# GpSimd's gathers wait for pair n - 10 in place of pair n - 16, in a two-pass graph kernel

## The chip, the cores and the metric

The kernel runs on one core of one Trainium2 chip. The metric is the device time of one execution in microseconds (us). Three runs of the kernel before are shown; their median is 2636.99 us. A pass of the kernel takes some 1250 us, so times of single waits are given to hundredths of a us.

## The reference, cut to what matters

Two graph layers run one after the other over 6250 nodes and 106250 edges, all vectors with 256 float32 elements. An edge has a source and a destination node; the edges are sorted by destination. Only the message part of each layer matters here:

```python
# layer 0, the first pass
msg = relu(x[src] + edge_attr)
agg = segment_sum(msg, dst)          # then a dense part per node, giving x
# layer 1, the second pass
h = gelu((x[src] + edge_attr) @ W1m + b1m)
agg = segment_sum(h @ W2m + b2m, dst) / max(degree, 1)   # then a dense part per node
```

## The kernel before, in words

**Tiling.** A group is 1024 edges: 8 tiles of 128, in 4 pairs of tiles. There are G = 104 groups, so M = 416 pairs; a pair is numbered n, and n = 4 g + j for pair j of group g. A round is 16 pairs. Both passes go over all pairs, and the code of each engine is written pair by pair: `first_pass(i, s)` and `second_pass(i, s)` hold what the engine does at pair 16 i + s, with the dense work on nodes (`node_a`, `node_b`) laid between the pairs by tables. The first rounds and the last ones are written out, those between are a loop.

**A pair in the first pass.** GpSimd gathers the 2 x 128 rows x[src] from memory into a slot of `m_all` with two indirect DMAs (`gather`, its instruction is L682), one for each tile; the first eight pairs take their indices from a list that is there early. SyncE loads the edges' attributes into `e_all` (L559). ScalarE copies them to a PSUM bank (L848). VectorE adds bank and gathered rows in place (`add_edges`, L1537) and raises the semaphore `added`. ScalarE applies the relu (L858). TensorE multiplies the two tiles by selection matrices to sum them by destination (`tile_sums`, L1141), and raises `pair_summed` by 2 after the pairs with j = 1 and j = 3. Beside it TensorE makes some of the second pass's products ahead (`ahead`, L1174), which ScalarE keeps (L867, L872). Who waits for `pair_summed` in this pass: ScalarE before it keeps these products and copies the sums (L918), VectorE before it makes the selection matrices of the group after the next in order (L1457) and before it adds a group's sums to `acc` (L1487), SyncE before it loads `ez` (L562), and GpSimd.

**A pair in the second pass.** GpSimd gathers rows of `y_scratch`, which the first pass has stored (y is x @ W1m + b1m of the new x), into the same slots. TensorE multiplies the edges' attributes by W1m (`product`, L1215) for j = 0, 1, 2 and raises `z_made` after each; for j = 2 (second tile) and j = 3 ScalarE copies stored products (`put_z`, L888). VectorE adds gathered rows to the bank (`add_rows`, L1560, raises `added`), ScalarE makes the gelu twice (L910, L911), VectorE the low part (L1566), and TensorE sums (`sums_split`, L1257), four pairs behind the products. `z_made` is waited for by VectorE's addition, by `put_z` and by SyncE's loads of edges (L540). Three pieces of products of the last groups are made early too, in this pass (`make_early`, L1227).

**The ring of gathered rows.** `m_all` has ROUND = 16 slots and one semaphore `m_in` for each. Before a gather of pair n goes into a slot, what was in it must have been used. In the first pass the slot is free when the sums of pair n - 16 are done; GpSimd waits for `pair_summed` >= n - 15. In the second pass the slot is free when pair n - 16 has been added; GpSimd waits for `added` >= M + n - 15. So up to sixteen pairs are gathered or in flight ahead of the sums (of the additions, in the second pass). The eight pairs 0 to 7 are gathered before the other lists are there, and pairs 8 to 15 without a wait for sums. At the start of the second pass GpSimd waits for the last y, and before pair 12 also for `xab_out` and `a_clear`, since the last slots are used by the dense work of the first pass.

**GpSimd's other work.** After the gathers of each pass it makes a few reciprocal square roots for the last nodes (`deviation`, L706 and L708). VectorE waits for them.

Of the kernel before, what the change touches and what calls it, by code (L numbers as in the profile page):

```python
# [23 lines left out]
BLK = 2  # L24

ROUND = 16
PER_ROUND = ROUND // PAIRS
ERING = 8
AHEAD = 3
# [57 lines left out]
def rounds(eng, body, first, stop, last):  # L87

    for i in range(first):
        for s in range(ROUND):  # L90
            body(i, s)
    with eng.Fori(0, stop - first) as r:
        for s in range(ROUND):
            body(r + first, s)
    for n in range(stop * ROUND, last + 1):
        body(n // ROUND, n % ROUND)


def groups(eng, body, first, stop):

    for i in range(first):
        for q in range(PER_ROUND):
            body(i, q)
    with eng.Fori(0, stop - first) as r:
        for q in range(PER_ROUND):
            body(r + first, q)


def known(n):
    return isinstance(n, int)  # L110


def build(nc, x, xT, src, dst, edge, edgeT, w1T, w2T, w1m, w2mT, w1u, w2u, vt, vr, out):
# [4 lines left out]
    M = G * PAIRS  # L118
# [9 lines left out]
    TURN = 512 - (KD + 1) * WIN  # L128
    assert P <= repeated < 2 * P and M == ROUND * ROUNDS and G > full and KH == 2 * KD and G <= P and CHUNK % 2 == 0 and N % 4 == 2
    assert ENDING < left and left - ENDING <= P  # L130

    chunks = [(c * CHUNK, CHUNK) for c in range(R)] + [(R * CHUNK, left - ENDING), (N - ENDING, ENDING)]

    need = [PER_ROUND * (c + 1) + 1 for c in range(R)] + [G - 1, G]
    LOOP_A, LOOP_B = (3, ROUNDS - 1), (4, ROUNDS - 1)
# [19 lines left out]
    def last_group(places, i, s):  # L155

        found = [G - LAST_SUMS + e for e, n in enumerate(places) if known(i) and n is not None and M + n == i * ROUND + s]
        return divmod(found[0], PER_ROUND) if found else None

    def ending(c):  # L160
        return known(c) and c >= R
# [20 lines left out]
    def groups_needed(c):  # L182
        return need[c] if known(c) else PER_ROUND * c + PER_ROUND + 1

# [14 lines left out]
    with ExitStack() as ctx:  # L199
# [134 lines left out]
        def small_b(c):  # L334
            return small_l if known(c) and c == R - 1 else small(c)
# [14 lines left out]
        def row(name, rows, blocks):  # L350
# [18 lines left out]
        added, act_made, act_high, act_low, z_made = map(sem, ("added", "act_made", "act_high", "act_low", "z_made"))  # L369
        sel_made, pair_summed, sum_copied, sum_turned, acc_done = map(  # L370
            sem, ("sel_made", "pair_summed", "sum_copied", "sum_turned", "acc_done"))
# [52 lines left out]

        ends_by_psum = PER_ROUND * (ROUNDS - 1)

# [73 lines left out]
        def tile_of(i, s):  # L500

            return 1 if known(i) and ROUND * i + s == M - PAIRS else 0
# [173 lines left out]
        @block.gpsimd  # L676
        def _(pool):
            def gather(table, sources, n, first=0):
                g, j = divmod(n, PAIRS)
                for t in range(first, 2):  # L680
                    u = 2 * j + t
                    pool.indirect_dma_start(  # L682
                        out=m_sb[n % ROUND][:, t, :], out_offset=None, in_=table,
                        in_offset=bass.IndirectOffsetOnAxis(ap=sources(g, u), axis=0),
                    ).then_inc(last_in if n == M - 1 and t == 0 else m_in[n % ROUND], 16)

            pool.iota(iota_i[:], pattern=[[1, WIN]], base=0, channel_multiplier=0).then_inc(consts_made, 1)
            pool.iota(place[:], pattern=[[1, 1]], base=0, channel_multiplier=1).then_inc(consts_made, 1)
            pool.memset(ident[:], 0.0).then_inc(consts_made, 1)
            pool.memset(eps[:], EPS).then_inc(consts_made, 1)  # L690
            pool.memset(root[:], -0.5).then_inc(consts_made, 1)
            pool.wait_ge(consts_made, 5)
            pool.affine_select(out=ident[:], in_=ident[:], compare_op=ALU.not_equal, fill=1.0, base=0,
                               pattern=[[-1, P]], channel_multiplier=1).then_inc(consts_made, 1)
            pool.wait_ge(src_first, 16)
            for n in range(2 * PAIRS):
                gather(x, lambda g, u: src_0[:, g, u:u + 1], n)
            pool.wait_ge(lists_made, 2)
            for n in range(2 * PAIRS, M):
                if n >= ROUND:  # L700
                    pool.wait_ge(pair_summed, n - ROUND + 1)
                gather(x, lambda g, u: src_p[:, u, g:g + 1], n)

            def deviation(m, rows, at, n):

                pool.tensor_tensor(m.ve[0:rows, at], m.mv[0:rows, at, 1], eps[0:rows, at], ALU.add).then_inc(eps_added, 1)  # L706
                pool.wait_ge(eps_added, n)
                pool.tensor_tensor(m.rs[0:rows, at], m.ve[0:rows, at], root[0:rows, at], ALU.pow).then_inc(rooted, 1)  # L708

            def deviation_x(e, at, steps, n):  # L710

                pool.wait_ge(x_dev[e], steps)
                deviation(small_x[e], chunks[R + e][1], slice(at, at + 1), n)

            rows = CHUNK // BLK
            pool.wait_ge(a_dev, DEV_A * (R - 1) + 2)
            deviation(small_n, rows, slice(0, BLK), 1)
            deviation_x(0, 0, 2, 2)
            deviation_x(1, 0, 2, 3)

            pool.wait_ge(lists_made, 4)
            pool.wait_ge(pair_summed, M)
            pool.wait_ge(y_out, 16 * C)
            for n in range(M):
                if n == 12:

                    pool.wait_ge(xab_out, 32 * C)
                    pool.wait_ge(a_clear, C)
                if n >= ROUND:
                    pool.wait_ge(added, M + n - ROUND + 1)  # L730
                gather(y_dram, lambda g, u: src_u[:, u, g:g + 1], n, tile_of(*divmod(n, ROUND)))

            for k, (c, second) in enumerate(roots):
                if ending(c):
                    deviation_x(c - R, second, 9 if second else 6, 4 + k)
                    continue
                pool.wait_ge(last_dev[c - R + 2], 5 if second else 2)
                at = slice(BLK, 2 * BLK) if second else slice(0, BLK)
                if c == R - 2 and second:
                    pool.wait_ge(b_o, c)  # L740
                elif c == R - 2:

                    pool.wait_ge(b_dev, DEV_B * (R - 2))
                    pool.wait_ge(b_o, c - 1)
                    at = slice(0, 2 * BLK)
                deviation(small_b(c), rows, at, 4 + k)
# [1162 lines left out]
```

## Time and profile before

| | us |
|---|---|
| median of the 3 runs (2627.64 to 2640.62) | 2636.99 |
| the profiled execution | 2636.03 |
| its span, first to last instruction | 2634.2 |
| busy: TensorE / GpSimd / VectorE / ScalarE | 2019.9 / 1593.8 / 1496.7 / 1290.4 |
| mean granted share of TensorE's clock | 0.898 |

The first pass runs from about 29 us to 1285 us of the span, the second from 1285 us to the end. In rows of the timeline the first number is the start, the second the time taken, then the engine (PE is TensorE, DVE VectorE, ACT ScalarE, POOL GpSimd, SPq the issuing of a DMA by SyncE), line, operation, what it writes and reads, shape and how many instructions were merged. In brackets stands how long the engine had been idle before it and what ended that wait; "remote" is a semaphore's update beside which the profile finds no instruction that had just ended, "issue" is no wait that the profile shows.

### The profile page before, as it was taken

The numbers are of one execution on the slowest core, as the hardware profiler recorded it, in microseconds if no ns is written. First come the engines' busy times: TensorE is split into PE (matmuls) and PEld (weight loads), VectorE is DVE, ScalarE is ACT, GpSimd is POOL, SyncE is SP. The second block draws the span as 40 slices with busy tenths as digits, with TensorE's granted clock in tenths as the row PEclk, the third lists the DMA queues.
The fourth block names the chain that finished last, engine by engine and source line by source line (L and its number), as shares of the span: only waits on it lengthen the run. The fifth ranks groups of instructions, "written<-read, shape, count | busy, mean of one in ns | idle before, by whom it ended". The sixth has DMA issues, their size and how long they took to land.

```text
span 2634.2 us, 38365 instructions
## 1 busy us (share of the span) xinstructions
PE 2019.9 (77%) x9090; PEld 1641.1 (62%) x9090; DVE 1496.7 (57%) x3743; ACT 1290.4 (49%) x2640; POOL 1593.8 (61%) x1695
## 2 busy tenths in 40 slices
PE   4787787877788777778647887878778778778877
PEld 3666666666666666666546666666666666666666
DVE  3455555455555555555434666666666666666666
ACT  4545545454555454544334445445445444454445
POOL 6666666666666666665466666666666656666561
PEclk8898988888888889989868989999999988999998
DMA  6788888888888888887556666666666656666662
GB/s 212 250 270 273 263 257 264 268 257 271 256 267 261 256 271 262 264 269 246 154 161 197 184 180 184 187 182 187 184 184 182 186 170 187 183 180 191 180 187 79
DMA packets 349113, 569.44 MB, mean 216 GB/s; under 512 B 48328, under 2 KB 214212, under 8 KB 349044
## 3 DMA queue, kind: packets, MB, share of 16 engines
q1 hardware_dynamic: 268858, 349.78, 43.3%
q0 software_dynamic: 79824, 218.08, 27.3%
q10 hardware_dynamic: 362, 0.85, 0.1%
q8 instruction: 19, 0.31, 0.0%
q14 instruction: 50, 0.41, 0.0%
HBM read 500.59 MB, written 67.94 MB: 216 GB/s over the span
## 4 chain that ended last, share of the span: by engine, by line
PE 39%; issue 18%; another core or an unknown queue 17%; DVE 16%; DVEq 5%; ACT 4%; DMA 1%; ACTq 0%; POOL 0%; POOLq 0%
PE bank L1141 12%; PE bank L1215 7%; PE bank L1174 6%; DVE m_lo L1566 4%; PE bank L1257 3%; PE bank L1049 3%; DVE sel L1457 2%; DVE m_all L1537 2%; PE bank L1123 2%; PE bank L1112 2%; DVE bank L1560 2%; DVEq L1493 1%; PE bank L1089 1%; ACT m_all L858 1%
## 5 line engine op out<-in xcount | busy, mean ns | idle before, releaser
L682 POOL DMA_INDIRECT m_all<-y_scratch,src_u x831 | 790.0, 951 | 499.4 <-DVE bank L1560 250.9
L682 POOL DMA_INDIRECT m_all<-in_x,src_p x816 | 777.3, 953 | 436.0 <-issue 217.5
L1141 PE MATMUL bank<-m_all,sel 128*128 128x257 f32 x1632 | 494.3, 430 | 139.9 <-ACT m_all L858 78.5
L1560 DVE TENSOR_TENSOR bank<-bank,m_all 128x512 f32<-128x512 f32 x415 | 288.6, 695 | 484.1 <-remote 387.1
L1215 PE MATMUL bank<-w1m_sb,e_all 128*128 128x256 f32 x2040 | 542.6, 409 | 4.5 <-DVE m_all L1680 2.5
L1141 PEld LDWEIGHTS bank<-m_all,sel 128*128 128x128 f32 x1632 | 332.0, 212 | 227.6 <-issue 157.6
L1257 PE MATMUL bank<-m_lo,sel 128*128 128x256 f32 x824 | 283.1, 364 | 231.4 <-DVE sel L1457 125.5
L1174 PE MATMUL bank<-w1m_sb,ez 128*128 128x256 f32 x1236 | 357.1, 415 | 124.5 <-issue 121.1
L1215 PEld LDWEIGHTS bank<-w1m_sb,e_all 128*128 128x128 f32 x2040 | 401.6, 208 | 56.2 <-issue 3.2
L910 ACT ACTIVATE m_hi<-bank 128x512 fp32r<-128x512 f32 x412 | 246.0, 597 | 354.7 <-DVE bank L1560 174.3
L858 ACT ACTIVATE m_all<-m_all 128x512 f32<-128x512 f32 x415 | 261.1, 629 | 246.4 <-DVE m_all L1537 139.7
L1174 PEld LDWEIGHTS bank<-w1m_sb,ez 128*128 128x128 f32 x1236 | 249.5, 208 | 197.8 <-issue 161.1
L1487 DVE TENSOR_TENSOR acc<-acc,bank 128x240 f32 (+1 forms) x208 | 75.2, 362 | 476.0 <-remote 223.1
L1257 PEld LDWEIGHTS bank<-m_lo,sel 128*128 128x128 f32 x824 | 169.7, 206 | 274.7 <-issue 211.5
L1537 DVE TENSOR_TENSOR m_all<-bank,m_all 128x512 f32<-128x512 f32 x415 | 282.2, 686 | 25.1 <-issue 9.8
L1566 DVE TENSOR_TENSOR m_lo<-bank,m_hi 128x512 fp32r<-128x512 f32 x412 | 281.0, 682 | 11.2 <-ACT bank L911 7.2
L888 ACT COPY bank<-e_all 128x256 f32<-128x256 f32 (+1 forms) x212 | 101.6, 479 | 319.1 <-remote 247.3
L911 ACT ACTIVATE bank<-bank 128x512 f32<-128x512 f32 x412 | 244.2, 593 | 0.0
L848 ACT COPY bank<-e_all 128x512 f32<-128x512 f32 x416 | 241.8, 582 | 0.9 <-issue 0.9
L1257 PE MATMUL bank<-m_hi,sel 128*128 128x256 f32 x824 | 229.4, 298 | 0.4 <-issue 0.4
L867 ACT COPY zc<-bank 128x512 f32<-128x512 f32 x103 | 60.4, 586 | 335.5 <-remote 157.6
L1257 PEld LDWEIGHTS bank<-m_hi,sel 128*128 128x128 f32 x824 | 171.6, 208 | 4.4 <-issue 0.6
(200 smaller groups left out, 2121.2 us busy)
## 6 DMA issues: line engine op xcount, KB each, us to landing
e_all<-in_edge SPq DMA_DIRECT2D x416, 256.0 KB
e_all<-in_edgeT SPq DMA_DIRECT2D x204, 256.0 KB
ez<-in_edgeT SPq DMA_DIRECT2D x103, 384.0 KB
z_scratch<-zc SPq DMA_DIRECT2D x103, 384.0 KB
e_all<-z_scratch SPq DMA_DIRECT2D x103, 256.0 KB
m_all<-y_scratch,src_u POOLq DMA_INDIRECT x831
e_all<-z_scratch SPq DMA_DIRECT2D x103, 128.0 KB
m_all<-in_x,src_p POOLq DMA_INDIRECT x816
```

The costliest lines, as they stand in the source:

```text
L682: pool.indirect_dma_start(out=m_sb[n % ROUND][:, t, :], out_offset=None, in_=table, in_offset=bass.IndirectOffsetOnAxis(ap=sources(g, u), ...
L848: act.copy(e_bank(s)[:], e_all[:, s % ERING, :]).then_inc(e_moved, 1)
L858: act.activation(m_sb[s], m_sb[s], ACT.Relu).then_inc(act_made, 1)
L910: act.activation(hi, z, ACT.Gelu).then_inc(act_high, 1)
L911: act.activation(z, z, ACT.Gelu).then_inc(act_made, 1)
L1141: return pe.matmul(psum[:, 0:D + 1], selection[:, u, :].bitcast(F32), m_all[:, slot, u % 2, 0:D + 1], start=(u == 0), stop=(u == TILES - 1 ...
L1174: last = pe.matmul(ahead_bank[a // 2][:, a % 2 * D:(a % 2 + 1) * D], ez_sb[q % 2][:, k, a * P:(a + 1) * P], w1m_sb[:, k, :], start=(k == 0 ...
L1215: last = pe.matmul(z_bank(s)[:, t * D:(t + 1) * D], eT_sb[s % ERING][:, k, t * P:(t + 1) * P], w1m_sb[:, k, :], start=(k == 0), stop=(k == ...
L1257: last = pe.matmul(bank[q % 2][:, 0:D], sel[q % 2][:, u, :], part[s % ZBANKS][:, t * D:(t + 1) * D], start=(u == 2 * j + tile_of(i, s) and ...
L1537: dve.tensor_tensor(m_sb[s], e_bank(s)[:].rearrange("p (t d) -> p t d", d=D), m_sb[s], ALU.add).then_inc(added, 1)
L1560: dve.tensor_tensor(z if in_place else m, z, m, ALU.add).then_inc(done, 1)
L1566: dve.tensor_tensor(lo, z, hi.bitcast(F32), ALU.subtract).then_inc(act_low, 1)
```

## The change

A constant LEAD = 10 takes ROUND's place in GpSimd's two waits. The ring stays at 16 slots, and no other engine's code is touched. A gather of pair n now waits for `pair_summed` >= n - 9 in the first pass and for `added` >= M + n - 9 in the second, from pair 10 on.

```diff
 ROUND = 16
+LEAD = 10
...
             for n in range(2 * PAIRS, M):
-                if n >= ROUND:
-                    pool.wait_ge(pair_summed, n - ROUND + 1)
+                if n >= LEAD:
+                    pool.wait_ge(pair_summed, n - LEAD + 1)
                 gather(x, lambda g, u: src_p[:, u, g:g + 1], n)
...
-                if n >= ROUND:
-                    pool.wait_ge(added, M + n - ROUND + 1)
+                if n >= LEAD:
+                    pool.wait_ge(added, M + n - LEAD + 1)
                 gather(y_dram, lambda g, u: src_u[:, u, g:g + 1], n, tile_of(*divmod(n, ROUND)))
```

## Rows read from the trace of the kernel before

**Rows 1.** The page, busy time of each engine (share of the span), count.

```profile
PE 2019.9 (77%) x9090; PEld 1641.1 (62%) x9090; DVE 1496.7 (57%) x3743; ACT 1290.4 (49%) x2640; POOL 1593.8 (61%) x1695
```

**Rows 2.** Waits, first pass (100 to 1250 us): total us, times, longest.

```profile
DVE acc L1487 <- remote: 223.1, 48, 7.1
```

**Rows 3.** Waits, second pass (1350 to 2600 us): total us, times, longest.

```profile
DVE bank L1560 <- remote: 345.2, 92, 6.5
```

**Rows 4.** Timeline of the second pass's middle: TensorE, VectorE, GpSimd.

```profile
1810.21 1.89 PE L1215 MATMUL bank<-w1m_sb,e_all 128*128 128x256 f32 x8
...
1816.76 0.70 DVE L1560 TENSOR_TENSOR bank<-bank,m_all 128x512 f32<-128x512 f32 x1 [3.10 <-remote]
```

**Rows 5.** Timeline of the second pass's start: GpSimd's gathers.

```profile
1285.59 2.03 POOL L682 DMA_INDIRECT m_all<-y_scratch,src_u  x1 [3.10 <-DMA y_scratch<-m_all]
...
1319.30 0.95 POOL L682 DMA_INDIRECT m_all<-y_scratch,src_u  x1 [0.30 <-issue]
...
1321.80 0.95 POOL L682 DMA_INDIRECT m_all<-y_scratch,src_u  x1 [0.30 <-issue]
...
1338.05 0.95 POOL L682 DMA_INDIRECT m_all<-y_scratch,src_u  x1 [0.30 <-issue]
1345.90 0.94 POOL L682 DMA_INDIRECT m_all<-y_scratch,src_u  x1 [6.91 <-DVE bank L1560]
```

**Rows 6.** The same stretch: TensorE, VectorE, SyncE, ScalarE.

```profile
1297.21 0.70 DVE L1560 TENSOR_TENSOR bank<-bank,m_all 128x512 f32<-128x512 f32 x1 [2.97 <-DMA m_all<-y_scratch,src_u]
...
1300.46 0.70 DVE L1560 TENSOR_TENSOR bank<-bank,m_all 128x512 f32<-128x512 f32 x1 [0.24 <-issue]
...
1302.74 1.89 PE L1215 MATMUL bank<-w1m_sb,e_all 128*128 128x256 f32 x8
...
1316.23 29.08 SPq L540 DMA_DIRECT2D e_all<-in_edgeT  x2
...
1316.24 0.70 DVE L1560 TENSOR_TENSOR bank<-bank,m_all 128x512 f32<-128x512 f32 x1 [14.49 <-remote]
...
1344.93 0.70 DVE L1560 TENSOR_TENSOR bank<-bank,m_all 128x512 f32<-128x512 f32 x1 [27.41 <-remote]
```

**Rows 7.** Windows: us, busy of PE, PEld, DVE, ACT, POOL, granted clock, DMA share, GB/s.

```profile
100.00:1250.00 1150.00, 912.19 (x3772) 730.22 (x3770) 616.15 (x1684) 588.48 (x1207) 730.29 (x767) 0.89 0.82 263
...
1304.00:1316.00 12.00, 1.97 (x11) 1.43 (x10) 0.00 (x0) 0.00 (x0) 8.96 (x10) 0.75 0.35 101
```

**Rows 8.** Timeline of the end of the second pass: GpSimd, TensorE, VectorE.

```profile
2570.87 0.95 POOL L682 DMA_INDIRECT m_all<-y_scratch,src_u  x1 [0.30 <-issue]
...
2583.32 1.89 PE L1215 MATMUL bank<-w1m_sb,e_all 128*128 128x256 f32 x8
...
2585.24 0.70 DVE L1560 TENSOR_TENSOR bank<-bank,m_all 128x512 f32<-128x512 f32 x1 [0.59 <-PE bank L1215]
...
2588.94 0.19 POOL L706 TENSOR_TENSOR ve_n<-mv_n,eps 121x4 f32<-121x4 f32 x1 [17.12 <-DVE mv_n L1574]
```

**Rows 9.** Timeline of the first pass's start: GpSimd, TensorE, VectorE.

```profile
29.55 0.94 POOL L682 DMA_INDIRECT m_all<-in_x,src_p  x1 [3.67 <-DVE src_p L1432]
...
43.28 1.03 PE L1141 MATMUL bank<-m_all,sel 128*128 128x257 f32 x4
...
47.15 2.05 PE L1174 MATMUL bank<-w1m_sb,ez 128*128 128x256 f32 x4 [2.84 <-ACT zc L867]
...
50.59 1.03 PE L1174 MATMUL bank<-w1m_sb,ez 128*128 128x256 f32 x4
...
53.38 0.95 POOL L682 DMA_INDIRECT m_all<-in_x,src_p  x1 [0.30 <-issue]
...
57.69 0.32 DVE L1457 TENSOR_TENSOR sel<-iota,rel_p 128x160 fp32r<-128x160 f32 x1 [15.86 <-remote]
...
58.91 2.08 PE L1141 MATMUL bank<-m_all,sel 128*128 128x257 f32 x4 [7.30 <-ACT m_all L858]
```

**Rows 10.** Timeline of the first pass's middle: VectorE and GpSimd.

```profile
622.07 0.41 DVE L1487 TENSOR_TENSOR acc<-acc,bank 128x240 f32 x1 [5.07 <-PE bank L1141]
...
622.20 0.95 POOL L682 DMA_INDIRECT m_all<-in_x,src_p  x1 [2.10 <-PE bank L1141]
```

**Rows 11.** Timeline of the first pass's end: GpSimd's last gather and first deviation.

```profile
1238.22 0.95 POOL L682 DMA_INDIRECT m_all<-in_x,src_p  x1 [0.30 <-issue]
1268.33 0.19 POOL L706 TENSOR_TENSOR ve_n<-mv_n,eps 121x2 f32<-121x2 f32 x1 [29.17 <-DVE mv_n L1574]
```

## The prediction, made before the result was known

> **What bounds the kernel now.** I read the page first: TensorE is busy 77% of the span, GpSimd 61%, VectorE 57% [rows 1]. No engine is full, so the waits matter. The waits by pair of engines name the two places where VectorE stands: the adding of a group's sums in the first pass, 223.1 us in 48 waits [rows 2], and the addition in the second pass, 345.2 us in 92 waits [rows 3]. Both are ended by "remote", a semaphore's update with no instruction ending beside it. The addition waits for gathered rows or for `z_made`, TensorE's signal, so I looked at the timeline for which. The product before the addition at 1816.76 had run by 1812.10 (1810.21 + 1.89), 4.66 us earlier [rows 4].
>
> The start of the second pass shows it largest. TensorE's product of pair 5 had run by 1304.63 (1302.74 + 1.89), but VectorE's addition of pair 5 started at 1344.93 after 27.41 us idle; pair 4's came at 1316.24 after 14.49 us idle, and at 1316.23 SyncE issued the load that waits for the same count of `z_made` and for no gather [rows 6]. Its second load of that row ended at 1345.31, with the addition of pair 5. So both waited for TensorE's signal, not for rows. From 1304 to 1316 VectorE and ScalarE did nothing at all, TensorE was busy 1.97 us, DMA 0.35, where the first pass has 0.82 on average: nothing was short of an engine or of bandwidth [rows 7]. What ran was GpSimd: 43 gathers without a pause from 1285.59 to 1339.00 (1338.05 + 0.95), one each 1.25 us [rows 5]. The signal came 5.91 us after the last. At the end of the second pass the opposite is seen: GpSimd's last gather ended at 2571.82, and then a product that ended at 2585.21 (2583.32 + 1.89) released the addition at 2585.24, 0.03 us later [rows 8]. My reading: **while GpSimd issues gathers back to back, TensorE's completion signals are held, and they come when it pauses**. In the middle of the first pass GpSimd's pause was 2.10 us and ended with VectorE's wait, at 622.20 and 622.07 [rows 10]. The ring being full is what makes GpSimd pause.
>
> **The change part by part.** No instruction is added; 406 waits of each pass compare with a later count. GpSimd's queue holds only gathers and the deviations, so what stands behind each wait is the next gather and, at the ends, the deviations.
>
> Steady state, cost 0. In the second pass GpSimd sits at the limit and issues pair n + 10 where it issued pair n + 16, at the same moment, the addition of pair n; in the first pass the counts rise by 2 at the same moments and each still frees two pairs (10 and 16 are both even). The two gathers a pair, their pauses and what these hold are only renumbered, so each group keeps its waits of [rows 2] and [rows 3]. The cover for it is that rows land in time. At the second pass's start pair 1's second gather was issued some 5 us after the first start, at 1285.59 + 4.96 = 1290.55, and its rows were waited for until 1297.21 [rows 5, 6]: 6.7 us. With ten ahead, the tightest pair is the second of four that follow a release in the first pass: issued by 5 us after it (4 x 1.25), used in the next group, a pause and 8 gathers later (8 x 1.25 + 2.1 = 12.1 us) plus VectorE's way to its second pair. That leaves at least 7 us + 4 us against 6.7. If it failed, each missing microsecond would count 104 times in a pass.
>
> Start of the second pass. VectorE's additions of pairs 0 to 3 are done by 1301.16 (1300.46 + 0.70), before the new limit is met, so up to pair 13 nothing changes: 28 gathers, the 28th at 1319.30, ended at 1320.25 [rows 5, 6]. Pair 4's addition, at 1316.24, frees pair 14: two more, ended at 1322.75 [rows 5]. In place of 1339.00 GpSimd pauses at 1322.75. Held signals then come after 2.1 us as in the middle [rows 10], or 5.9 as here: at 1324.9 to 1328.7, against 1344.93. That is 16.2 to 20.0 us less. I take 17, near this stall's own row. If gathers don't hold the signals it is 0; a signal not held at all would give 40 (1344.93 - 1304.63). These are the ends.
>
> Start of the first pass. GpSimd issues pairs 8 to 17 from 29.55 to 54.33. TensorE's sums of pair 3 ended at 44.31, and VectorE, waiting for them, went on at 57.69: 13.4 us held [rows 9]. With ten ahead only pairs 8 and 9 are free, four gathers to about 34.5, and the sums of pairs 0 to 3 are signalled with GpSimd idle or just resumed. VectorE goes on at about 44.3. But of the 13.4 us TensorE used some for group 1: its three steps from 47.15 to 51.62 (50.59 + 1.03) take 4.5 us [rows 9] and now run first, to 44.3 + 4.5 = 48.8 plus what ScalarE's copy needs, some 49. The next sums then start at 49 in place of 58.91: 10 us less. The ends: 0 and 13.4.
>
> Ends of the passes. The last twelve gathers (six pairs) of each pass now go out about 18 us later (six pairs at 3 us), into a stretch where GpSimd was silent. First pass: silent from 1239.17 until the deviation at 1268.33, which it awaited for 29.17 us [rows 11]; the gathers end some 15 to 20 us later, so the deviation isn't late, but one or two signals are held, up to 4.7 us as in [rows 4] each. Second pass: silent from 2571.82 to 2588.94, 17.12 us [rows 8]; the last gather waits for the tenth pair from the end, and pair 405's addition is the one at 2585.24, so two gathers, to about 2588.4. This just clears the deviation. Signals held there: up to 6 us in all. I take 2.5 us at each end, bounds 0 and 5, 0 and 6.
>
> A page speaks against this change. The Trainium skill, "DMA: Bandwidth & Descriptors", section Rules for kernel authors, says to issue a DMA early and to wait for it late, so that its fixed cost is covered; cutting the lead can by this only lose. By that rule the two start terms are nil and what is left is the tightest pair's margin, which the second rival below prices.
>
> **Sum.** -17 - 10 + 2.5 + 2.5 = -22 us against the profiled execution's own 2636.03: 2614. That execution is 0.96 us under the median of 2636.99. Bound by bound: 2636.0 - 40 - 13.4 = 2583, and 2636.0 + 11 = 2647.
>
> **The rivals.** (1) The start stalls have another cause, and nothing moves: 2636. For it: pair 4's signal came at 1316.2 in the midst of the gathers [rows 6], so a pause isn't all that frees them. Against it: 13.4 us held at one start and 40 at the other, both with long runs of gathers, and 0.03 us where there are none [rows 5, 6, 8, 9]. Chance 0.17.
>
> A rule that leads here: the Trainium skill, "GPSIMD Engine Reference", section Key points, has GpSimd contend with VectorE for its interfaces to the on-chip memory. VectorE was idle while signals were held [rows 7], so that rule explains neither stall, and by it the gathers, at 0.95 us each, would run as before.
>
> (2) Slower: the shorter lead uncovers the landing of gathers at the second pair of the first pass's groups. It decides from a landing time of about 11 us. 6.7 us was seen where DMA was busy 0.35; in the first pass it is busy 0.82 [rows 7]. 0.5 us uncovered in each of 104 groups is 52 us, which with the forecast's -22 gives 2636 + 30 = 2666; a quarter of it, 13 us, would leave 2627. Together with both ends at their bounds of 11 and no gain, 2647, this side has a chance of 0.09.
>
> (3) Better: a held signal depends on how many gathers are in flight, and steady waits shrink too. If a tenth of the 568.3 us of [rows 2, 3] went, 57 us more: 2557. For it nothing is seen but the length of the first holds; chance 0.06.
>
> **How the numbers follow.** My forecast, the two starts shorter, has 0.68. A measurement of this kernel can tell about 0.5%, 13.2 us, from no change: below 2623.8 is faster, above 2650 slower. Of the 0.68, 0.62 lies under 2623.8 and 0.06 within; with (3) that is 0.68 faster. (1) and the milder half of (2) are within: 0.06 + 0.17 + 0.02 = 0.25. Slower 0.07. The range for 8 in 10: down to 2592 (the starts give 30 to 40), leaving (3) out, and up to 2638, which takes in (1) and leaves most of (2) out.
>
> **What would show it.** GpSimd's first pause in the second pass at about 1322 less the first pass's gain, and VectorE's long wait of 27.41 us cut to about 10. In the first pass's start, VectorE's wait of 15.86 us cut to 3 or so. Group period in both middles as before, waits of [rows 2, 3] within a few per cent. No wait of an addition that a gather's landing ends. If the long wait at the second start stays at 27 us although GpSimd has paused, the reading of the signals is wrong; if the middles are shorter or longer by over 1%, "only renumbered" is wrong.

## The result and the profile after

The changed kernel takes 2614.26 us, median of 5 runs (2606.17 to 2622.54), against 2636.99 us for 5 runs of the kernel before (2627.64 to 2640.71). The ratio is 0.9913, with a 95% interval of 0.9894 to 0.9932. The profiled execution took 2613.03 us, its span is 2611.2 us. The forecast was 2614.

The page's first part answers to [rows 1]: the same instructions and, within 1%, the same busy times. TensorE's is 19 us longer, GpSimd's 4 us, the span 23 us shorter.

```profile
PE 2039.1 (78%) x9090; PEld 1651.4 (63%) x9090; DVE 1498.9 (57%) x3743; ACT 1288.9 (49%) x2640; POOL 1598.1 (61%) x1695
```

**Second pass's start**, the timeline of GpSimd, against [rows 5]. The lines of this kernel are one higher than before (L683 for L682, L1561 for L1560).

```profile
1267.67 2.03 POOL L683 DMA_INDIRECT m_all<-y_scratch,src_u  x1 [3.11 <-DMA y_scratch<-m_all]
...
1305.20 0.95 POOL L683 DMA_INDIRECT m_all<-y_scratch,src_u  x1 [0.30 <-issue]
1311.81 0.95 POOL L683 DMA_INDIRECT m_all<-y_scratch,src_u  x1 [5.66 <-DVE bank L1561]
```

The same stretch on TensorE and on VectorE, against [rows 6]:

```profile
1285.59 1.89 PE L1216 MATMUL bank<-w1m_sb,e_all 128*128 128x256 f32 x8
...
1297.51 0.70 DVE L1561 TENSOR_TENSOR bank<-bank,m_all 128x512 f32<-128x512 f32 x1 [13.21 <-remote]
...
1310.84 0.70 DVE L1561 TENSOR_TENSOR bank<-bank,m_all 128x512 f32<-128x512 f32 x1 [12.04 <-remote]
```

GpSimd issued 30 gathers in a row (15 pairs) where it had issued 42 (21 pairs), and stopped at 1306.15 (1305.20 + 0.95). TensorE's product of pair 5 had run by 1287.48 (1285.59 + 1.89). Its signal came with the addition at 1310.84: held 23.4 us where it had been 40.3, and 4.7 us after the last gather. Pair 4's signal came at 1297.5, in the midst of the gathers, as it had before. From the first gather to the addition of pair 5 it is 43.2 us (1310.84 - 1267.67), where it was 59.3 (1344.93 - 1285.59).

**First pass's start**, GpSimd and VectorE, against [rows 9]:

```profile
33.03 0.95 POOL L683 DMA_INDIRECT m_all<-in_x,src_p  x1 [0.30 <-issue]
42.31 0.95 POOL L683 DMA_INDIRECT m_all<-in_x,src_p  x1 [8.33 <-PE bank L1142]
...
44.67 0.33 DVE L1458 TENSOR_TENSOR sel<-iota,rel_p 128x160 fp32r<-128x160 f32 x1 [2.67 <-PE bank L1142]
```

GpSimd stands still for 8.33 us, the sums' signal comes at once, and VectorE waits 2.67 us where it had waited 15.86.

**Middle of the first pass**, GpSimd and VectorE, against [rows 10]: a pause that ends with VectorE's wait, as before.

```profile
619.12 0.40 DVE L1488 TENSOR_TENSOR acc<-acc,bank 128x240 f32 x1 [4.33 <-PE bank L1142]
...
619.25 0.95 POOL L683 DMA_INDIRECT m_all<-in_x,src_p  x1 [2.00 <-PE bank L1142]
```

**Ends of the passes**, GpSimd's last gathers and what follows, against [rows 11] and [rows 8]: 

```profile
1233.09 0.95 POOL L683 DMA_INDIRECT m_all<-in_x,src_p  x1 [0.30 <-issue]
1250.41 0.20 POOL L707 TENSOR_TENSOR ve_n<-mv_n,eps 121x2 f32<-121x2 f32 x1 [16.38 <-DVE mv_n L1575]
...
2566.04 0.95 POOL L683 DMA_INDIRECT m_all<-y_scratch,src_u  x1 [0.30 <-issue]
2567.22 0.20 POOL L707 TENSOR_TENSOR ve_n<-mv_n,eps 121x4 f32<-121x4 f32 x1 [0.23 <-DVE mv_n L1575]
```

A table by places shows where the 23 us went. It takes the start of VectorE's additions (one record in 416 is missing in each pass, so the places may be off by one pair, the same in all profiles). The last two columns are single executions of two kernels of the experiments, both from one job on chip 10: lead 16 (start_fill_b, below) and lead 10 (lead10_again).

| stretch, us | before | after | lead 16, chip 10 | lead 10, chip 10 |
|---|---|---|---|---|
| first pass, to the 16th addition | 82.8 | 73.1 | 82.1 | 72.2 |
| 32nd to 384th addition, for a group | 11.88 | 11.73 | 11.75 | 11.78 |
| 400th to the last addition | 47.3 | 51.2 | 48.0 | 51.6 |
| second pass, first gather to pair 5's addition | 59.3 | 43.2 | (other start) | 43.1 |
| 32nd to 384th addition, for a group | 12.50 | 12.59 | 12.71 | 12.70 |
| 400th addition to the end | 65.6 | 65.3 | 66.5 | 66.6 |

### The profile page after: what moved, and what is told of

Same layout as the page of the kernel before. It is cut to its first block, busy times and chain, and to the rows that moved or that the text cites. A ratio compares the mean times of both kernels' runs of the same rounds, so it can differ in the third digit from the quotient of the medians.

```text
span 2611.2 us, 38365 instructions
## 1 busy us (share of the span) xinstructions
PE 2039.1 (78%) x9090; PEld 1651.4 (63%) x9090; DVE 1498.9 (57%) x3743; ACT 1288.9 (49%) x2640; POOL 1598.1 (61%) x1695
## 4 chain that ended last, share of the span: by engine, by line
PE 49%; issue 16%; another core or an unknown queue 13%; DVE 12%; ACT 6%; DVEq 4%; DMA 1%; ACTq 0%; POOL 0%; POOLq 0%
PE bank L1142 14%; PE bank L1216 10%; PE bank L1175 7%; PE bank L1258 4%; PE bank L1050 3%; DVE m_lo L1567 3%; PE bank L1113 2%; ACT m_all L859 2%; DVE sel L1458 2%; PE bank L1124 2%; PE bank L1090 2%; DVE bank L1561 1%; DVE m_all L1538 1%; ACT bank L912 1%
## 5 line engine op out<-in xcount | busy, mean ns | idle before, releaser
L683 POOL DMA_INDIRECT m_all<-y_scratch,src_u x831 | 792.3, 953 | 510.2 <-DVE bank L1561 271.7
L683 POOL DMA_INDIRECT m_all<-in_x,src_p x816 | 779.0, 955 | 428.9 <-issue 217.4
L1142 PE MATMUL bank<-m_all,sel 128*128 128x257 f32 x1632 | 485.3, 424 | 139.2 <-ACT m_all L859 73.1
L1216 PE MATMUL bank<-w1m_sb,e_all 128*128 128x256 f32 x2040 | 576.2, 426 | 19.7 <-issue 17.2
L1561 DVE TENSOR_TENSOR bank<-bank,m_all 128x512 f32<-128x512 f32 x415 | 288.2, 694 | 424.9 <-remote 203.6
L1216 PEld LDWEIGHTS bank<-w1m_sb,e_all 128*128 128x128 f32 x2040 | 419.7, 218 | 81.3 <-issue 22.8
```

What stands on the lines that cost most here:

```text
L683: pool.indirect_dma_start(out=m_sb[n % ROUND][:, t, :], out_offset=None, in_=table, in_offset=bass.IndirectOffsetOnAxis(ap=sources(g, u), ...
L1142: return pe.matmul(psum[:, 0:D + 1], selection[:, u, :].bitcast(F32), m_all[:, slot, u % 2, 0:D + 1], start=(u == 0), stop=(u == TILES - 1 ...
L1216: last = pe.matmul(z_bank(s)[:, t * D:(t + 1) * D], eT_sb[s % ERING][:, k, t * P:(t + 1) * P], w1m_sb[:, k, :], start=(k == 0), stop=(k == ...
L1561: dve.tensor_tensor(z if in_place else m, z, m, ALU.add).then_inc(done, 1)
```

## The experiments

The kernels of a job ran on one chip, beside the kernel before. The five jobs came to five chips, and these fall into two kinds: on chips 10 and 8 the kernel before took 2637 and 2650 us, on chips 12, 14 and 4 it took 2152, 2147 and 2147 us. The chip of the result above is of the first kind. Nothing here can be read without that. The kernels of job 1, with the change in one pass or in the starts alone, ran on a chip of the second kind and were not run on one of the first, so the split of the gain by places rests on the traces.

**Job 1, chip 12.** Three kernels place the change in one pass or in the starts:

```diff
# first_only: the first pass's wait alone; second_only: the second's alone
-                    pool.wait_ge(pair_summed, n - ROUND + 1)
+                    pool.wait_ge(pair_summed, n - LEAD + 1)
# starts_only, both waits
+def lead(n):
+    return min(ROUND, 10 + 2 * (max(0, n - 24) // 16))
```

> LEAD = 10 in the first pass alone, 16 in the second. Theory (gathers issued back to back hold TensorE's signals, and each place gives its own share): the first pass ends about 18 us earlier, as in the changed kernel (there 1285.59 became 1267.67), half of it from the start (10 us) and the rest from a group period of 11.73 in place of 11.88 us; the second pass starts as before, with 43 gathers in one run and VectorE's long wait of about 27 us. Time about 2637 - 18 = 2619. Rival (the two passes are not separable, the second start's stall depends on what the first pass leaves): the long wait changes too. Rival (the shorter period is drift between executions): period 11.88, time about 2630.

> LEAD = 10 in the second pass alone. Theory: the first pass as before (ends at about 1285), VectorE's fifth and sixth additions of the second pass as in the changed kernel, the sixth about 43 us after the first gather in place of 59, so 16 us less there; the middle of the second pass no faster, perhaps 0.1 us a group slower (10 us in all) as the changed kernel's profile shows. Time between 2637 - 17 = 2620 and 2637 - 5 = 2632. Rival (the 10 us lost in the second pass's middle is drift): 2620.

> A lead of 10 for the first 40 pairs of each pass, then two more every 16 pairs, up to 16 from pair 72 on; so only the starts are changed. Theory (the starts alone carry the gain that was forecast): 10 us less at the first start and 17 at the second, the first pass's middle back at 11.88 us a group, the ends as before: 2637 - 27 = 2610. Rival (the first pass's shorter period of 11.73 us is from the lead in the steady state and carries 13 us; the second pass's middle loses 10 with lead 10): then this one keeps the second and misses the first, 2637 - 27 = 2610 as well, but the period in the profile is 11.88 against 11.73 us, which tells them apart.

The fourth keeps the lead at 16 and breaks up the row of gathers with other work on GpSimd:

```diff
                 gather(y_dram, ..., n, tile_of(*divmod(n, ROUND)))
+                if n < ROUND and n % 2:
+                    for k in range(3 * (n - 1), 3 * (n + 1)):
+                        pool.tensor_tensor(spare[:, k:k + 1], eps[:, 0:1], root[:, 0:1], ALU.pow)
```

> Lead 16 everywhere as before, but in the first sixteen pairs of the second pass GpSimd does six small powers (about 0.55 us each, 3 us) after every fourth gather, with results that nobody reads. Theory (it is the issuing of gathers back to back that holds the signals, not how far ahead they are): the signals come in these breaks; VectorE's additions of pairs 4 and 5 come within about 10 us of the products, the wait of 27 us is gone, and the time falls by 15 to 30 us, to 2607 to 2622, although GpSimd has 24 us more to do. Rival (the hold ends only when GpSimd really waits, or depends on the count of gathers ahead): the stall stays at 27 us or grows by the 24 us of added work, time 2637 to 2660.

Against 2152.20 us of the kernel before: first_only 2158.67, ratio 1.0036 (1.0024 to 1.0048); second_only 2150.59, 0.9993 (0.9984 to 1.0002); starts_only 2158.99, 1.0031 (1.002 to 1.0042); start_fill 2176.41, 1.0115 (1.01 to 1.0131). None of the expected gains came. The profile of second_only says why. Two products and the additions behind them at the second pass's start, and a row of the windows of the first pass's middle:

```profile
1086.96 1.89 PE L1216 MATMUL bank<-w1m_sb,e_all 128*128 128x256 f32 x8
1089.16 1.89 PE L1216 MATMUL bank<-w1m_sb,e_all 128*128 128x256 f32 x8
```

```profile
1088.88 0.70 DVE L1561 TENSOR_TENSOR bank<-bank,m_all 128x512 f32<-128x512 f32 x1 [0.55 <-PE bank L1216]
1091.09 0.70 DVE L1561 TENSOR_TENSOR bank<-bank,m_all 128x512 f32<-128x512 f32 x1 [0.91 <-PE bank L1216]
```

```profile
150.00:1000.00 850.00, 717.42 (x3293) 570.31 (x3292) 553.41 (x1476) 514.44 (x1056) 644.05 (x677) 0.99 0.94 311
```

The products of pairs 4 and 5 end at 1088.85 and 1091.05, with gathers going out every 1.25 us, and the additions start 0.03 and 0.04 us later. On this chip no signal is held. The two waits that [rows 6] show at 14.49 and 27.41 us are 0.55 and 0.91. GpSimd then never pauses in the middle: a group takes 10.02 to 10.10 us in both passes, which is 8 gathers of 1.25 us. The granted clock is 0.99, where before the middle of the first pass has 0.89 [rows 7]. What VectorE waits for most is the landing of rows (209.1 us in 199 waits from 150 to 1000 us), where the first kind shows none. So GpSimd's issuing is the bound, and each us in which it stands still is lost. With lead 10 in the first pass it does so once, as first_only's timeline of GpSimd shows:

```profile
39.94 0.95 POOL L683 DMA_INDIRECT m_all<-in_x,src_p  x1 [8.96 <-PE bank L1142]
```

8.96 us in place of the usual 0.30 is 8.7 us, against 6.5 us between the medians and 7.7 by the ratio. second_only has no such stop and costs nothing. start_fill agrees: a break takes 3.36 us from gather to gather (3.16 of powers, 0.02 and 0.18 around them) in place of 0.30, eight of them are 24.5 us, and it is 24.2 us slower.

**Job 2, chip 10.** The changed kernel itself, start_fill again, and a lead of 8:

> The changed kernel once more, beside the kernel before on the same chip. On the chip of the four runs so far the kernel before took 2152 us and no signal of TensorE was held (0.01 to 0.02 us from the end of the sums to the update), GpSimd issued without a pause, 10.02 us a group, and so GpSimd is the bound. Theory: what the change does depends on whether the signals are held. If this chip holds them (kernel before about 2637 us), the change gains about 20 us, ratio 0.991. If it doesn't (kernel before about 2152 us), the lead of 10 only stops GpSimd for some 8.7 us at the first pass's start, where it waits for the sums of pair 1, and the ratio is 1.003 to 1.005. Rival (the held signals are a matter of the kernel's build, not of the chip): ratio 0.991 on either.

> The kernel with lead 16 and 3 us of small powers on GpSimd after every fourth gather of the second pass's first sixteen pairs, once more. On a chip that doesn't hold the signals it cost 24 us, as much as the added work, since GpSimd is the bound there. On a chip that holds them (kernel before about 2637 us), theory (issuing back to back holds them): the sixth addition comes in one of the breaks and the wait of 27 us is gone, 15 to 30 us faster. Rival (only a GpSimd that waits lets them through): no faster, up to 24 us slower.

```diff
-LEAD = 10
+LEAD = 8
```

> LEAD = 8 in both passes. On a chip that holds the signals: 4 gathers fewer in the second start's first run, so the sixth addition comes 4 x 1.25 = 5 us earlier than with 10, the rest as with 10, or lost again if rows now land late: ratio about 0.989, with landing waits in the first pass 0.995 or more. On one that doesn't: GpSimd stops at the first start as with 10, about 1.004, and more if the sums, up to two groups behind, now stop it in the middle, which would show as a pause and a group period over 10.02 us.

This chip holds the signals. Against 2636.82 us: lead10_again 2614.93, ratio 0.9916 (0.9895 to 0.9936), the result once more; lead8 2613.21, 0.9908 (0.9886 to 0.993); start_fill_b 2654.16, 1.0057 (1.0037 to 1.0078).

start_fill_b missed its time and made its point. GpSimd's row of gathers with the breaks, and VectorE's additions from pair 2 on:

```profile
1291.92 1.00 POOL L683 DMA_INDIRECT m_all<-y_scratch,src_u  x1 [0.18 <-issue]
1293.23 0.95 POOL L683 DMA_INDIRECT m_all<-y_scratch,src_u  x1 [0.30 <-issue]
1294.48 0.95 POOL L683 DMA_INDIRECT m_all<-y_scratch,src_u  x1 [0.30 <-issue]
1295.73 0.95 POOL L683 DMA_INDIRECT m_all<-y_scratch,src_u  x1 [0.30 <-issue]
1296.71 3.16 POOL L735 TENSOR_TENSOR spare<-eps,root 128x1 f32<-128x1 f32 x6
1300.05 1.00 POOL L683 DMA_INDIRECT m_all<-y_scratch,src_u  x1 [0.18 <-issue]
```

```profile
1288.82 0.70 DVE L1564 TENSOR_TENSOR bank<-bank,m_all 128x512 f32<-128x512 f32 x1 [1.34 <-DMA m_all<-y_scratch,src_u]
1291.17 0.70 DVE L1564 TENSOR_TENSOR bank<-bank,m_all 128x512 f32<-128x512 f32 x1 [0.92 <-DMA m_all<-y_scratch,src_u]
1296.15 0.70 DVE L1564 TENSOR_TENSOR bank<-bank,m_all 128x512 f32<-128x512 f32 x1 [3.69 <-DMA m_all<-y_scratch,src_u]
1298.70 0.70 DVE L1564 TENSOR_TENSOR bank<-bank,m_all 128x512 f32<-128x512 f32 x1 [1.25 <-DMA m_all<-y_scratch,src_u]
...
1381.99 0.70 DVE L1564 TENSOR_TENSOR bank<-bank,m_all 128x512 f32<-128x512 f32 x1 [27.55 <-remote]
```

Two of the products:

```profile
1292.16 1.89 PE L1219 MATMUL bank<-w1m_sb,e_all 128*128 128x256 f32 x8
...
1342.15 1.03 PE L1219 MATMUL bank<-w1m_sb,e_all 128*128 128x256 f32 x4
```

With the ring and the lead of before, and only the row of gathers cut into fours by 3 us of other work, the eleven signals of products from 1291.86 to 1341.86 (the first of the two above at 1294.06, for an end at 1294.05) come within 0.02 us of the product's end. The addition of pair 5 starts 24.3 us after the first gather (1298.70 - 1274.43), against 59.3 with lead 16 and 43.1 with lead 10, and what ends VectorE's waits is now the landing of rows. So breaking the row is enough to let the signals by. GpSimd was also less far ahead here (15 gathers begun and 6 pairs added at 1302.92, against 15 and 4 at 1304.63 in the kernel before), so this run alone doesn't part the two. The middles do: there the kernel before has GpSimd at its limit, 16 pairs ahead. Where TensorE's work ended over 2.5 us after a row's last gather, all 6 signals came at once, and 21 of 28 where it ended 1.5 to 2.5 us after; and leads of 8, 10 and 16 have the same group in the first pass on this chip, 11.74, 11.78 and 11.75 us. It is the unbroken issuing that holds the signals, not how far ahead GpSimd is. Nor need GpSimd wait: it was busy in these breaks. But rows now come late, and when the breaks stop after pair 15, GpSimd, at 1340.62 and far from its limit, issues gathers without a pause to beyond 1389. The product that ended at 1343.18 (1342.15 + 1.03) is signalled at 1381.96, 38.8 us later: the stall has only moved. From the 16th addition (1339.25) to the 32nd it is 85.5 us, where the kernel before has 49.1 (1421.74 - 1372.62). The release at 1381.96 came in the midst of the gathers, as pair 4's did, so a pause is not the only thing that frees a signal.

lead8 gives the size for the second start. GpSimd stops at 1302.00, 4 gathers earlier, and goes on after 5.03 us:

```profile
1301.05 0.95 POOL L683 DMA_INDIRECT m_all<-y_scratch,src_u  x1 [0.30 <-issue]
1307.02 0.94 POOL L683 DMA_INDIRECT m_all<-y_scratch,src_u  x1 [5.03 <-DVE bank L1561]
...
1306.05 0.70 DVE L1561 TENSOR_TENSOR bank<-bank,m_all 128x512 f32<-128x512 f32 x1 [7.87 <-remote]
```

The addition of pair 5 is at 37.5 us from the first gather (1306.05 - 1268.59), 5.6 less than with 10, where 5 were expected. By pair 63 less is left: it is added 217.8 us after the first gather, against 222.1 in lead10_again on the same chip and 218.9 in the kernel of the result. The medians of lead 8 and lead 10, 2613.21 and 2614.93, do not differ beyond their scatter.

**Jobs 3 and 4, chips 14 and 8.** If a held signal costs only a short gap, a gap could be put into the steady state. Two kernels, each sent twice:

```diff
+            def pause():
...
+                pool.tensor_tensor(spare[:, k % 64:k % 64 + 1], eps[:, 0:1], root[:, 0:1], ALU.pow).then_inc(spared, 1)
# pow4: behind every fourth gather. set2: a memset of that column in its place, behind every pair
+                if n % 2:
+                    pause()
```

> The changed kernel (lead 10) with one small power on GpSimd (about 0.5 us) after every fourth gather, in both passes. On a chip that holds the signals (kernel before about 2637 us) the delay of the release after a run of gathers was 2.0, 4.7 and 5.9 us for runs of 8, 31 and 43 gathers, some 0.1 us for each gather. Theory (a backlog builds up while gathers are issued, some 0.1 us each, and signals stand behind it): 0.48 us after every four gathers is enough to work it off, signals pass at once, the first pass's group falls from 11.75 us to what GpSimd needs, 8 x 1.25 + 2 x 0.48 = 11.0, and the second's from 12.6 to about 11.0: 2615 - 104 x 0.75 - 104 x 1.6 = 2370. Rival (the signals need a pause of about 2 us, whatever came before): nothing passes in the breaks, and the added 0.96 us a group stands in the first pass's loop: 2615 + 100 = 2715, in the second pass between 0 and 100 more. On a chip that doesn't hold them (kernel before 2152 us) both expect 2152 + 200 = 2352.

> The changed kernel with one tiny write on GpSimd (a column of 128 elements, about 0.1 us) after every pair's two gathers, in both passes. Any break in the row of gathers that would let signals by without costing time: if another instruction on GpSimd is enough, whatever its length, both passes fall to about 10.4 us a group, 2615 - 104 x 1.3 - 104 x 2.2 = 2250. By the theory of the backlog a tiny write that fits into the 0.30 us between gathers gives it no time, and nothing changes but for its own cost: 2615 to 2640. On a chip that doesn't hold the signals it costs only its own time, 0 to 0.2 us a pair, 2152 to 2320.

On chip 14, which holds nothing (2147.47 us): pow4 2369.15, 1.1027 (1.1006 to 1.1047), and set2 2156.44, 1.004 (1.0026 to 1.0054). The 412 powers cost 222 us, 0.54 us each, the lead's own cost included, and the 824 tiny writes nothing that shows beside it (first_only had 1.0036 on chip 12): they fit between two gathers. That is GpSimd as the bound again.

> The changed kernel with one small power after every fourth gather, once more. The runs on a chip that doesn't hold the signals gave 2369 us and groups of 11.18 and 11.10 us: that is what GpSimd alone needs for it. If this chip holds them (kernel before about 2637 us): theory (backlog of about 0.1 us a gather, worked off in 0.5 us after every four): signals pass, and the time is the same 2370. Rival (a pause of about 2 us is needed): the loop of the first pass is 11.1 us + 2.0 us = 13.1 us a group, 2615 + 104 x 1.35 = 2755, the second pass not faster either. If the chip doesn't hold them: 2369 again.

> The changed kernel with one tiny write after every pair's gathers, once more; it costs nothing in the row of gathers (the write takes 0.12 us of the 0.30 us between two gathers). If this chip holds the signals: a mere other instruction on GpSimd lets them pass, 2160 to 2250; by the backlog theory it gives no time for them and nothing changes, 2610 to 2630. If it doesn't: 2156 again.

On chip 8, which holds them (2649.87 us): pow4_b 2638.33, 0.9957 (0.994 to 0.9974), and set2_b 2635.23, 0.9949 (0.9931 to 0.9966). A tiny write does not bring the gain of 350 us or more that was to be expected if it let the signals by. Lead 10 alone was not run on this chip, so what the powers and the writes cost there is not known. pow4_b answers neither theory: no gain of 250 us, no loss of 140. Its timeline of GpSimd in the first pass's middle:

```profile
600.41 0.95 POOL L684 DMA_INDIRECT m_all<-in_x,src_p  x1 [0.30 <-issue]
601.38 0.59 POOL L696 TENSOR_TENSOR spare<-eps,root 128x1 f32<-128x1 f32 x1
602.90 0.99 POOL L684 DMA_INDIRECT m_all<-in_x,src_p  x1 [0.93 <-remote]
```

From that row's last gather (ended 601.36) to the next gather it is 1.5 us, where the kernel of the result has 2.00, and a group takes 12.01 us in place of 11.73: 8 gathers, one break inside the row and the rest of the wait. The break inside, 0.78 us from gather to gather in the median, let almost nothing pass in the steady state: in 1 of 88 such breaks from 150 to 1200 us an update of TensorE's sums or products came. At the second pass's start it did sometimes: VectorE's waits there were 2.68, 4.41, 14.05 and 6.56 us. A theory in which 0.5 us for every four gathers works off the whole backlog has fallen.

Put together over the six profiles of holding chips with plain or nearly plain rows of gathers (before, after, lead10_again, lead8, start_fill_b, set2_b), counting for each record of TensorE with an update when the semaphore's next recorded update came. At once is within 0.06 us of the work's end. Late is an update after that and before the next work on the same semaphore ended, so surely this one's. The last column has no update of its own in that time: held past the next one, or not recorded.

| the work ended | at once | late | can't be told |
|---|---|---|---|
| in the first 5 us of a row of gathers | 553 | 367 | 488 |
| further in | 54 | 1240 | 779 |
| up to 1.5 us after the row's last gather | 64 | 808 | 76 |
| 1.5 to 2.5 us after | 202 | 70 | 3 |
| over 2.5 us after | 306 | 0 | 0 |

The last column can't be counted as held, because on these chips many updates of every engine have no record: `added` has 348 update times for 832 additions in the kernel before, and 833 in second_only on chip 12. That VectorE's signals got through is seen at who waits for them. In the second pass of the kernel before, ScalarE, idle until then, started within 0.06 us of the end of VectorE's addition in 146 of 153 cases in which that addition ended within a row of gathers. So it is TensorE's signals that are held, not all. Of the late ones, 2130 came while GpSimd paused and 355 while gathers were being issued.

Where a signal from within a row came late and after the row, the first of them came, in the median, 0.9 us after the last gather of a row of 2 (82 rows), 1.1 of 4 (76), 1.5 of 6 (33), 1.75 of 8 (620), 2.0 of 10 (97), 2.3 of 12 (24), and at the second pass's starts 4.05 us after 26 gathers (lead8), 4.7 after 30 and 5.9 after 42: about 0.7 us and 0.12 to 0.13 us for each gather.

**Job 5, chip 4.** The last run was to use this for the second start, with a short first row.

```diff
-                if n >= LEAD:
-                    pool.wait_ge(added, M + n - LEAD + 1)
+                if n >= 2 * PAIRS:
+                    pool.wait_ge(added, M + n - lead(n) + 1)
# with lead(n) = min(LEAD, max(4, 2 + n // 4))
```

> The changed kernel, but the lead in the second pass's start grows from four: pair 8 waits for the addition of pair 4, pair 12 for that of 7, pair 16 for that of 10, and so on up to ten from pair 32. Theory (signals come 1 us plus about 0.1 us for each gather of the run after GpSimd pauses, so the first run's length sets the first stall): the first run has 16 gathers in place of 31 (it ends about 21 us after its start) and the release comes 1 + 1.6 = 2.6 to 3 us after it, so the sixth addition comes about 24 us after the first gather, where it was 43.2 us in the changed kernel and 37.5 us with lead 8. That is 19 us less than with 10; some of it is lost in the next pairs, whose rows are gathered only then (5 us at most): on a chip that holds the signals ratio to the kernel before (2637 - 22 - 14 to 19) about 0.985. Rival (the first stall only moves to the next pairs, since the same sums and gathers have to be done): the sixth addition is early, but pair 15's addition is at most a few us earlier than the 70.3 us of the changed kernel, ratio 0.991. On a chip that doesn't hold them the change to the ramp costs nothing, ratio 1.004 as with the lead of ten.

The chip was one that doesn't hold signals: 2155.52 us against 2147.10, ratio 1.0039 (1.0025 to 1.0053). As expected there, the ramp adds nothing to what the lead of ten costs. What it does on a chip that holds them was not measured.

## Why the prediction was right, and where by luck

- **The reading of the waits** held. Signals of TensorE are held while GpSimd issues gathers back to back, and come when it stops: start_fill_b shows it by breaking the row, and the middles of the passes show that the lead's length is not what holds them. What the prediction could not know is that this is so on some chips only. On the others its first rival, that nothing moves at the starts, is nearly what happens, and kernels with lead 10 in the first pass were 0.3 to 0.4% slower. The changed kernel itself was not run on such a chip. That the forecast of 2614 met 2614.26 to a fraction of a us is luck: the five executions lie between 2606 and 2623.
- **Second start, -17**: -16.2 to the addition of pair 5, with a release 4.7 us after the last gather, inside the 2.1 to 5.9 that were taken as bounds. The prediction's count of the row is one too high: 42 gathers ran before, not 43, and the gather at 1319.30 is the 27th, not the 28th. So the pause of its own rule comes at 1324.00 and not at 1322.75, and its span for the term becomes 15.0 to 18.8 us in place of 16.2 to 20.0. After the change the pause came 38.5 us after the first gather, as 1324.07 would be before, and the 17 taken holds by either count.
- **First start, -10**: -9.8 at the 16th addition, and -10.0 between the two kernels on chip 10.
- **Steady state, 0**: right, though the two profiles alone seem to deny it. The first pass's middle is 12 us shorter and the second's 12 us longer in the changed kernel. On chip 10 a lead of 16 and one of 10 have 11.75 and 11.78 us a group in the first pass; in the second the kernels with those leads in force have 12.71 and 12.70. By the prediction's own sign, a middle longer or shorter by over 1%, the first pass's (11.88 to 11.73, 1.2%) speaks against "only renumbered"; the pair on chip 10, 0.2% apart, does not bear it out. So the middles most likely differ between executions, not by the lead, though each is one execution; here the two differences cancelled, which is luck for the single profile and not needed for the medians. The waits of [rows 2] stayed in sum, 414 us before and 425 after from 100 to 1230 us for VectorE's `acc` behind TensorE's sums and "remote", 450 and 446 with those ended by L1135 (L1136 after). Those of [rows 3] did not stay within a few per cent as foretold, but shifted between releasers: from 1400 to 2500 us the part ended by "remote" fell from 309.6 to 141.2 us, while the group took no less.
- **End of the first pass, +2.5**: +3.9, and +3.5 on chip 10. Which signals make it up was not followed.
- **End of the second, +2.5**: nothing (-0.2 and +0.1). This is the one term whose step fails: no net time was lost to signals held by the last gathers. The deviation was not delayed, but stands only 0.23 us behind the last gather's row, where it had 17.12 us.
- **The sum**: with chip 10's terms for all but the second start it is -10.0 - 16.2 + 3.5 + 0.1 = -22.6 us, and the medians there differ by 21.9. This is the forecast's -22, with no term off by more than 2.4 us. The second start's term is borrowed from the result's chip, since no profile of the kernel before is kept from chip 10.
- **The rivals.** Rows did not land late on chips that hold the signals (VectorE's addition has one wait of 3.2 us for them in the whole second pass, 3.0 before), so the slower rival had no part. It names what is true on the other chips, in another form: there GpSimd must not stand still at all.
- **The Trainium skill** ("DMA: Bandwidth & Descriptors", Rules for kernel authors) spoke against waiting longer before a transfer is issued. On chips 12, 14 and 4 the kernels with the shorter lead in the first pass side with it, 1.0031 to 1.004, though what they lose is GpSimd's one stop and not a landing laid bare; the lead in the second pass alone cost nothing there (0.9993). On those that hold the signals the ratios of 0.9913 and 0.9916 go against it. The Trainium skill's "GPSIMD Engine Reference", Key points, which names contention with VectorE for two kinds of its instructions, was named as no explanation of the stalls, and no run gives it a part: a gather takes 0.95 us on either kind of chip, whether VectorE is idle or busy.

## What to carry to other kernels

When a wait ends on a semaphore's update and the instruction that should have raised it ended long before, look at what another engine was doing in between, here rows of gathers. A shorter lead is then no loss and can be a gain, because it cuts the first, longest row; but the gain lies at the starts, and the steady state, where the row's length is set by the loop and not by the ring, stays as it is. Measure on several chips before such a change is kept: kernels with it in the first pass lost 0.3 to 0.4% on three chips of five, and it gained 0.8% on chip 10 and 0.9% on the chip of the result.

## What the hardware did that was not expected

- The same program takes 2637 or 2650 us on two chips and 2147 to 2152 us on three others, 19% less. On those three nearly all of TensorE's updates come at once while gathers are issued (in second_only 805 of 806 within 0.06 us), and a group takes 10.02 us, GpSimd's eight gathers. On the two they are held, and it takes 11.7 to 12.7. Each chip was seen in one job, so it is open whether it is the chip itself or something of its state.
- TensorE's granted clock is 0.99 in the first pass's middle on chip 12, and 0.88 to 0.90 in the profiles before, after, lead10_again and set2_b of those that hold the signals. There TensorE also stands still more, 679 us busy of 850 before against 717 in second_only.
- The two kinds of chip differ in the trace too: the kernel before has 2990 recorded update times for the 6568 updates that its engines' instructions make, second_only has one for each. A missing record of an update is no sign that it was held; the start of the instruction that waits for it is.
- Held signals are mostly let go in a gap of GpSimd of about 0.7 us plus 0.12 to 0.13 us for each gather before it, and some without one (355 of 2485; the long ones at the starts after 12 to 39 us). What in the chip holds them was not found.
- A write of 128 elements on GpSimd between two indirect DMAs is free where GpSimd is the bound: set2 with 824 of them has 1.004 on chip 14, and kernels without them have as much, first_only on chip 12 (1.0036) and the ramp on chip 4 (1.0039).
